# An early-fusion block in eight pairs of images: half of the gate on GpSimd, one rotation for three token tiles, narrower key windows, new orders

## What is computed

```
h = concat(cls, patches @ W_lin + b, txt) (+ positions)             # 16 x 165 x 256
q, k, v = rope(n @ Wq), rope(n @ Wk), n @ Wv      n = layernorm(h)  # 16 query heads, 4 key heads, 16 wide
scores = q k / 4, where |i - j| <= 32, else -inf  ; h += softmax(scores) v @ Wo
xq = int8 per token of layernorm(h);  w1, w2 to -1, 0, 1 times a scale
u = conv3(xq @ w1)  (3 taps along the tokens, 1024 channels)
g = silu(u);  h += (int8 per token of g) @ w2
```

## Time and profile before

| | us |
|---|---|
| three runs | 435.99, 437.55, 438.02 (median 437.55) |
| profiled execution, own time | 435.96 |
| its span | 434.2 |
| DVE busy | 313.8 (72%) |
| ACT busy | 277.2 (64%) |
| POOL busy | 219.7 (51%) |
| PE busy (ends modelled) | 357.3 (82%) |

### The profile page before, as it was taken

How to read it: one execution, slowest core, us unless ns; L and a number is a source line. 1 busy time by engine, 2 the same in 40 slices (tenths; PEclk the granted TensorE clock), 3 DMA queues, 4 the chain that set the end, 5 groups by cost and what they waited for, 6 DMA issues and landing times.

```text
span 434.2 us, 8318 instructions
## 1 busy us (share of the span) xinstructions
PE 357.3 (82%) x2920; PEld 274.9 (63%) x2920; DVE 313.8 (72%) x644; ACT 277.2 (64%) x523; POOL 219.7 (51%) x244
## 2 busy tenths in 40 slices
PE   1683998997999697998997799899998998936533
PEld 1452776776787486667775687688667766824423
DVE  1147548754599766887897689859976997899972
ACT  2240356776788755876976698679757966661812
POOL 2306379698389623994499309961983016010000
PEclk9998899997899989999999999999999999985956
DMA  8671051000000010001000100010001000000011
GB/s 232 154 169 24 19 203 27 1 18 10 2 1 2 2 39 22 18 17 33 2 13 14 33 0 11 17 33 0 19 10 31 2 2 15 20 2 0 0 32 31
DMA packets 17788, 13.86 MB, mean 32 GB/s; under 512 B 10109, under 2 KB 16698, under 8 KB 17747
## 3 DMA queue, kind: packets, MB, share of 16 engines
q1 hardware_dynamic: 16852, 12.18, 10.9%
q10 hardware_dynamic: 895, 1.16, 1.0%
HBM read 7.91 MB, written 2.70 MB: 24 GB/s over the span
## 4 chain that ended last, share of the span: by engine, by line
POOL 37%; PE 27%; DVE 11%; issue 10%; ACT 5%; DMA 5%; SPq 3%; POOLq 0%; ACTq 0%; DVEq 0%
POOL qkr L1064 7%; POOL rsn L1059 5%; POOL rc L1057 5%; POOL shared L1084 5%; POOL qsp L1076 5%; PE bank L1635 3%; POOL qsp L1072 3%; SPq L996 3%; PE bank L1842 2%; PE bank L1821 2%; DMA cst<-in_consts 2%; POOL shared L1092 2%; POOL qsp L1073 2%; PE bank L1736 2%; POOL rs L1035 2%
## 5 line engine op out<-in xcount | busy, mean ns | idle before, releaser
L1190 ACT COPY pT<-bank 94x480 f32<-94x480 f32 x88 | 49.0, 557 | 20.1 <-PE bank L1754 20.0
L1408 DVE TENSOR_REDUCE mx<-bank 120x4 fp32r<-120x376 f32 x88 | 47.2, 542 | 18.2 <-PE bank L1736 18.2
L1736 PE MATMUL bank<-kbd,q_hl 128*120 128x376 f32 x176 | 57.2, 410 | 0.0
L1754 PE MATMUL bank<-cst,pr 120*94 120x120 f32 x352 | 52.1, 270 | 2.7 <-ACT pT L1190 1.7
L1035 POOL TENSOR_TENSOR rs<-ve,half_neg 110x3 f32<-110x3 f32 x16 | 15.4, 962 | 75.2 <-DVE ve L1436 43.5
L1182 ACT ACTIVATE pr<-bank 120x376 f32<-120x376 f32 x88 | 42.7, 488 | 16.2 <-PE bank L1744 15.4
L1226 ACT ACTIVATE shared<-bank,conv 128x330 f32<-128x330 f32 x64 | 39.4, 633 | 12.3 <-PE bank L1822 11.5
L1821 PE MATMUL bank<-xT_hi,w1T 128*128 128x330 f32 x128 | 45.4, 360 | 2.1 <-DVE shared L1491 1.7
L1484 DVE SCALAR_TENSOR_TENSOR shared<-bank,conv,shared 128x328 f32<-128x328 f32 x64 | 35.3, 555 | 13.9 <-ACT shared L1226 13.2
L1754 PEld LDWEIGHTS bank<-cst,pr 120*94 120x94 f32 x352 | 37.6, 126 | 11.0 <-issue 5.2
L1042 POOL TENSOR_SCALAR xn<-h,mv,rs 110x256 f32<-110x256 f32 x21 | 29.0, 1387 | 25.6 <-PE bank L1674 25.1
(11 more groups left out here) (120 smaller groups left out, 854.8 us busy)
## 6 DMA issues: line engine op xcount, KB each, us to landing
out<-h SPq DMA_DIRECT2D x8, 330.0 KB
wn<-in_w SPq DMA_DIRECT2D x2, 1024.0 KB, 6.7
shared<-in_x SPq DMA_DIRECT2D x4, 432.0 KB
vw<-qk SPq DMA_DIRECT2D x40, 23.5 KB
h<-in_txt SPq DMA_DIRECT2D x1, 770.0 KB
wlT<-in_lin SPq DMA_DIRECT2D x1, 768.0 KB, 7.2
h<-tokp SPq DMA_DIRECT2D x14, 36.0 KB
h<-in_txt SPq DMA_DIRECT2D x1, 448.0 KB
```

The costliest lines, as they stand in the source:

```text
L1190: nc.scalar.copy(pT[:, g % 3, :], PT_BANK[0:KW, 0:HKV * QP]).then_inc(p_kept, 1)
L1408: nc.vector.tensor_reduce(mx[:, g % 4, :].bitcast(F32R), S_BANKS[g % 2][0:QP, 0:HKV * KW].rearrange("p (k c) -> p k c", k=HKV), axis=AX.X, ...
L1736: o = nc.tensor.matmul(dst, q_hl[n % 2][:, j * QB:(j + 1) * QB, :].bitcast(F32R), kbd[n % 2][:, part, :, k0:k0 + KW].bitcast(F32R), start= ...
L1754: o = nc.tensor.transpose(PT_BANK[0:KW, kv * QP:(kv + 1) * QP], pr[:, g % 3, kv * KW:(kv + 1) * KW], ident[0:QP, 0:QP])
```

## The change

1. **Gate.** The first half of `silu` leaves DVE. POOL makes it in two products over 128x1320, th*u and then that plus u. `abs_g` of the first half waits for POOL. The second half stays on DVE.
2. **Rotation.** From pair 1 on, one call of `rope` handles all three token tiles: 7 instructions of three times the columns in place of 21. It waits for the last `keep_qk`, and every `turn_q` waits for all of it. In pair 0 nothing changes (one tile on POOL, two on DVE).
3. **Keys.** Each block gets the keys that it can see: widths 62, 92, 94, 94, 78, 94, 78, 94, 94, 92, 62 in place of 94 (mean 84.9). The mask is added after the two products and only over the columns at the edges (29 to 94 of each key head, mean 56.2, so 225 in all).
4. **Orders.** Every row of `ORDER` and `ONCE` is new.

```
-            def rope(n, t):
...
+            def rope(n, ts, parts, added, high, split, before):
+                cnt = ts.stop - ts.start
...
+                pool.wait_ge(qk_kept, NT * n + ts.stop)
...
+                nc.gpsimd.tensor_tensor(rot[:, ts, :].rearrange("p t (h d) -> p t h d", h=heads), q_v, table(0), ALU.mult)
+                nc.gpsimd.tensor_tensor(swp[:, ts, :].rearrange("p t (h d) -> p t h d", h=heads), q_v, table(1),
+                                        ALU.mult).then_inc(parts, 1)
...
                 for e in range(2):
-                    o = nc.gpsimd.tensor_tensor(qkr[:, e::2], rc[:, e::2], rsn[:, 1 - e::2], ALU.add)
+                    o = nc.gpsimd.tensor_tensor(rot[:, ts, e::2], rot[:, ts, e::2], swp[:, ts, 1 - e::2], ALU.add)
...
+            def silu_first(n):
+                pool.wait_ge(tanhed, NP * n + 1)
+                nc.gpsimd.tensor_tensor(th[:, 0:HALFC, :], th[:, 0:HALFC, :], u[:, 0:HALFC, :], ALU.mult).then_inc(gate_mult, 1)
+                pool.wait_ge(gate_mult, n + 1)
+                nc.gpsimd.tensor_tensor(u[:, 0:HALFC, :], th[:, 0:HALFC, :], u[:, 0:HALFC, :], ALU.add).then_inc(gated_p, 1)
...
             def abs_g(n, p):
-                act.wait_ge(silued, NP * n + p + 1)
+                act.wait_ge(gated_v if p else gated_p, n + 1)
...
             def turn_q(n, t):
-                pe.wait_ge(q_split[t], n + 1)
+                if n:
+                    pe.wait_ge(q_split, n)
...
-                nc.tensor.matmul(dst, identb[0:QP, 0:QP], mask_v[:, j, :].unsqueeze(1).to_broadcast([QP, HKV, KW]),
-                                 start=True, stop=False)
                 for part in range(2):
-                    o = nc.tensor.matmul(dst, q_hl[n % 2][:, j * QB:(j + 1) * QB, :].bitcast(F32R),
-                                         kbd[n % 2][:, part, :, k0:k0 + KW].bitcast(F32R), start=False, stop=(part == 1))
+                    nc.tensor.matmul(dst, q_hl[n % 2][:, j * QB:(j + 1) * QB, :].bitcast(F32R),
+                                     kbd[n % 2][:, part, :, k0:k0 + w].bitcast(F32R), start=(part == 0), stop=(part == 1))
...
+                nc.tensor.matmul(over, identb[0:QP, 0:QP], hide,
+                                 start=False, stop=True, skip_group_check=True).then_inc(scored, 1)
```

More of the change, by code:

```diff
@@ L69, with keys_of, edges @@
 POSR = NPATCH + 1
-def key_start(j):
-    return min(max(QB * j - HALF_WINDOW, 0), T - KW)
+def keys_of(t):
+    lo = t // SEQ * SEQ
+    return max(t - HALF_WINDOW, lo), min(t + HALF_WINDOW + 1, lo + SEQ)
+SEEN = [[keys_of(t) for t in range(QB * j, QB * (j + 1))] for j in range(NB)]
+KEY0 = [min(lo for lo, hi in seen) // 2 * 2 if j < NB // 2 else min(lo for lo, hi in seen) for j, seen in enumerate(SEEN)]
+WIDTH = [-(-(max(hi for lo, hi in seen) - k0) // 2) * 2 for seen, k0 in zip(SEEN, KEY0)]
+def edges(j):
+    lo, hi = max(lo for lo, hi in SEEN[j]) - KEY0[j], min(hi for lo, hi in SEEN[j]) - KEY0[j]
+    if lo >= hi:
+        return 0, 1, WIDTH[j]
+    left, right = lo, WIDTH[j] - hi
+    if not left:
+        return hi, 1, right
+    if not right:
+        return 0, 1, left
+    return 0, 2, max(left, right)
+MASK_AT = [0]
+for _j in range(NB):
+    MASK_AT.append(MASK_AT[-1] + edges(_j)[1] * edges(_j)[2])
 def tok_pieces(s):
@@ L345 @@
-        (332,),
-        (369,),
+        (46,),
+        (89,),
+        (137,),
+        (184,),
+        (234,),
+        (280,),
+        (322,),
+        (359,),
     ),
     'dve.max_x': (
-        (48,),
-        (94,),
-        (143,),
-        (192,),
-        (242,),
-        (289,),
-        (338,),
-        (375,),
+        (51,),
+        (96,),
+        (145,),
+        (193,),
+        (239,),
+        (288,),
+        (331,),
+        (367,),
     ),
     'dve.low_x': (
-        (57,),
+        (56,),
@@ L360 @@
         (104,),
-        (152,),
-        (200,),
-        (249,),
-        (297,),
-        (345,),
-        (379,),
+        (153,),
+        (201,),
+        (247,),
+        (295,),
+        (342,),
+        (372,),
     ),
     'dve.left': (
[8 rows of a table removed]
[8 rows of a table added]
     ),
     'dve.right': (
[8 rows of a table removed]
[8 rows of a table added]
+    ),
+    'dve.fold_g': (
+        (74, 86),
+        (123, 134),
+        (174, 182),
+        (224, 230),
+        (268, 274),
+        (318, 325),
+        (364, 368),
+        (395, 397),
+    ),
+    'dve.max_g': (
+        (82, 87),
+        (131, 136),
+        (179, 183),
+        (225, 231),
+        (272, 278),
+        (319, 326),
+        (366, 369),
+        (396, 398),
@@ L447 @@
+        (194, 196, 197),
+        (241, 242, 243),
+        (289, 291, 292),
+        (337, 339, 340),
+        (385, 392, 393),
+        (402, 403, 404),
     ),
@@ L630 @@
         (4,),
+        (6,),
         (9,),
[L632 to L636 removed]
+        (15,),
+        (22,),
+        (29,),
+        (41,),
     ),
     'pool.rstd2': (
[L639 to L646 removed]
+        (11,),
+        (18,),
+        (25,),
+        (32,),
+        (37,),
+        (44,),
+        (48,),
+        (52,),
     ),
     'pool.norm2': (
[L649 to L655 removed]
+        (12,),
+        (19,),
+        (26,),
+        (33,),
+        (38,),
+        (45,),
+        (49,),
         (),
@@ L658 @@
     'pool.dequant_x': (
-        (17,),
-        (25,),
-        (33,),
-        (41,),
-        (48,),
-        (55,),
-        (58,),
-        (),
+        (13,),
+        (21,),
+        (27,),
+        (34,),
+        (40,),
+        (46,),
+        (50,),
+        (),
+    ),
+    'pool.silu_first': (
+        (16,),
+        (23,),
+        (30,),
+        (35,),
+        (42,),
+        (47,),
+        (51,),
+        (53,),
     ),
@@ L671 @@
         (7,),
-        (9,),
+        (10,),
+        (12,),
+        (14,),
+        (16,),
+        (18,),
+    ),
+    'sp.store': (
+        (8,),
         (11,),
@@ L710, in times_of @@
         return [(t, k) for k, t in enumerate(ONCE[name])]
-    return [(t, (n, k)) for n in range(PAIRS) for k, t in enumerate(ORDER[name][n]) if t is not None]
+    return [(t, (n, k)) for n, row in enumerate(ORDER[name]) for k, t in enumerate(row) if t is not None]
 TICKS = sorted({t for name in (*ORDER, *ONCE) for t, _ in times_of(name)})
@@ L1108, in _ @@
                     dequant_x(n)
-                for n, t in work["rope"].get(q, ()):
-                    rope(n, t)
+                for n, _ in work["rope"].get(q, ()):
+                    rope_pair(n)
+                for n, _ in work["silu_first"].get(q, ()):
+                    silu_first(n)
         @block.scalar
@@ L1586, in _ @@
                     right(n, m)
-                for n, p in work["silu"].get(q, ()):
-                    silu(n, p)
+                for n, _ in work["silu"].get(q, ()):
+                    silu(n, 1)
                 for n, p in work["fold_g"].get(q, ()):
```

688 lines of the change are left out of this document (323 added, 365 removed), and 176 rows, old and new, of the table ORDER.

## The result

The changed kernel takes **467.93 us** (median of four runs, 466.63 to 469.80) against 437.11 for the kernel before on the same chip: ratio 1.071, 95% interval 1.0664 to 1.0755. It is 30.8 us slower; 434.5 was forecast, in a range of 425 to 443. The span of the profiled execution is 466.2 us. Two kernels of the experiments, the rotation in 21 pieces and the one with the gate in pieces too, have one execution each in a slower state (466.49 and 474.74 us) in their medians.

The account below looks back on a forecast made before the run. No engine is full; POOL's rotation turns the chain, 42.3 us a turn. Terms +2.4 - 3.3 - 1.2 - 1.5 - 3.0 + 1.8 + 1.8 = -3.0 from 436.0 give 433.0, 434.5 on the median's scale; range 425 to 443.

Parts of the forecast that it names:

- load_v behind store: On SP, load_v(n+3) waiting behind store(n) costs 1 to 2 us at pair 5's copies, covered because the gate holds POOL.
- The other new orders I put at 0, between -2 and +2: The other new orders of the start, priced at 0, between -2 and +2 us.
- the convolution order: In the convolution of pairs 1 to 4, DVE works off fewer attention pieces: -1.8 us a turn, nothing if ACT doesn't keep up.
- Gate and rotation, +2.7 a turn before the offsets: On POOL, both together take 20.5 us in a turn that had 17.8; with offsets -1.0, +1.5 and -0.8, +2.4.
- Rival 1: POOL's queue is the turn and the convolution order gives nothing back: +9.6 instead of +2.4, 441.8 us; chance 0.26.
- rival 2: DVE instructions wait for longer POOL instructions to end: +1.2 us in five pairs, 440.5 us; chance 0.08.
- The merged rotation "3.5 of the 4.4" for DVE's work: On POOL, 3.5 of 4.4 us of hand-overs and stretching stay; with 11.0 for the merged call, 14.5 in place of 17.8.
- Pair 1's rotation, +1.8: The only rotation the scores wait for; merged, it ends 11.0 us after the last keep_qk instead of 4.5: +1.8, between 0 and 6.5.
- Keys, -4.5 in sum: Narrower keys shorten attention blocks: -3.3 us where attention is alone, -1.2 in the turns; gain between 0 and 17.6.
- Rival 4: The keys don't get cheaper: 4.5 us less gain, 439.0 us at most, 437 if half of it; chance 0.08.
- DVE, -4.5 for the lost gates: DVE loses eight gates: -1.5 us in pair 0's feed-forward part, -3.0 in pairs 5 and 6; bounds 0 and -12.2.
- The end, +1.8: In pair 7, the gate on POOL, despite an earlier tanh, delays the end: +1.8 us, bounds 0 and +3.5.

Follow-up runs that it names:

- the base: The changed kernel with SP's order of before (value copies of pair n+3 ahead of the store of pair n): 459.64 us, 1.0513 against the kernel before.
- experiment 6: Kernel before with new orders only up to the first turn_xs: 434.94 us; order edits on it (452.07) and on the changed kernel without its gate, rotation and SP edits (468.46, 445.13).

## Why the prediction was wrong

- **The step that failed** is the one that set new orders at nothing. In the prediction's words, load_v behind store "costs 1 to 2 us at that place, but the gate holds POOL until 264.4 anyway; cover: the gate". The length of the copies (12.7 us), their landing 2.0 after, and the wait that follows were right: 1.5 to 2.2 us in three of the four turns. What it holds was wrong: not only POOL, but ACT, and behind `keep_qk` on ACT the `mid` of the pair in its feed-forward part. The cover was named for one waiter out of two, the wait in the first of the four turns is 6.75, and the delay closes a ring through `add_ffn` and `store`. Price 8.3 us, not 0.
- **"The other new orders I put at 0, between -2 and +2"**, and the convolution order at -1.8 a turn. The -1.8 never came: in the base the last `right` of pairs 1 to 4 ends 22.7, 18.6, 18.9 and 17.5 us after `turn_xs`, before it was 21.0, 19.2, 18.0 and 18.8, on average 0.2 later. I counted what left the convolution and not where it went. The start gives 2.3 (shown). The rest of the orders costs some 15 (13 with the start's gain in it); of these 4.8 are the places of stats1 and of the gate on DVE, shown in a kernel whose gate is on DVE. About 10 stay open: in the four turns they lie mostly behind the last `right` (experiment 6), but no run took their causes apart, and the two that tried made it worse.
- **Gate and rotation, +2.7 a turn before the offsets.** The durations were right. Rival 1's mechanism, POOL's queue as the turn, is shown under the old orders (4.6 us for the gate alone in the turn that was read). In the changed kernel it isn't what turns: POOL has 9% of the chain. The 9.7 us of both are there all the same, and they go by DVE: 11.7 of the 13.9 us that four turns lose stand in six DVE instructions.
- **The lock, rival 2.** The mechanism is shown, and 6 us were too few: shorter instructions on POOL, with more work in sum, take 10.7 us from five turns, and 11.0 from the six DVE instructions in four of them. Those six take 6.8 us in pair 3 before and 9.4 in pair 3 after. I gave it 0.08 and treated it as a rival of the forecast, where it is a term in every turn.
- **The merged rotation "3.5 of the 4.4" for DVE's work.** It takes 12.9 to 14.0 us in the turns (14.5 forecast), 11.0 undisturbed in pairs 1 and 2 (11.0 forecast). Right.
- **Pair 1's rotation, +1.8.** Wrong in sign: `turn_xs(0)` stands at 109.5 in the base and at 111.2 with the rotation in tiles, so merging gains 1.7 there, or 0.5 with the gate on DVE (110.7 and 111.2).
- **Keys, -4.5 in sum.** Rival 4 has the time right (0.9995, an interval around 1) and the mechanism wrong. The instructions did get shorter (a score product takes 300 ns at 248 columns and 353 at 312, 410 before at 376), the path did not; why not even pair 0's attention gained (`turn_xs(0)` at 113.3 in place of 113.9) stays open.
- **DVE, -4.5 for the lost gates.** None of it shows: DVE's busy time rose by 1.3 in place of falling by some 15, and pairs 5 and 6 take 1.7 us more than before (65.9 against 64.2).
- **The end, +1.8.** From `turn_xs(7)` to the end of the span 40.4 us in place of 38.7: +1.7, the number right. The reason is in part luck: with the gate back on DVE in the new orders the end still takes 39.5 us, or 40.3 with the rotation in tiles too.
- **Signs to look for.** The lengths of the products and POOL's idle time between gate and rotation in pairs 1, 2 and 4 (8.0, 2.0 and 2.6 us, and 2.7 in pair 3 too): right. POOL above 60%: wrong, 51% (its 239.4 us would be 55% of the forecast span). The chain through POOL: wrong, 9%. Turns of 42 to 43.5: wrong, 50 to 53.

No single rival was the result. In the order in which the experiments took it apart, it is the sum of a ring that I saw and priced at nothing (8.3), gate and rotation (9.7), and orders whose cost I did not look for (13, with the start's gain).

## What to carry to other kernels

When a step is put behind another in an in-order queue, follow every waiter of what it issues, on each engine, to what stands behind it, and ask whether the way leads back to the step it now waits for: that is a ring, and while it is closed no turn is shorter than it. Fewer, longer instructions on GpSimd save fixed cost (11.0 us against 13.0 for the same rotation with little beside it), and here they held VectorE longer (11.0 us in four turns) and handed over later: look at what VectorE does beside them before merging. Take a large reordering apart by stretches before judging it: here the first 110 us were a gain and the rest a loss.

## What the runs showed of the hardware

- DVE and POOL stretch each other in both directions. The rotation in 21 pieces takes 13.0 us in pair 2 and 15.1 in pair 1, where DVE works on 128x2048 elements beside it (1.29 and 1.76 us) and the three low parts take 4.54 in place of 2.49; in seven instructions it is 11.0 in both pairs. A 128x660 fold on DVE takes 0.84 to 2.81 us by what POOL does beside it.
- GpSimd's product is close to linear in columns over the range seen: 320 in 0.87, 960 in 2.16 to 2.24, 1320 in 2.96 to 3.00.
- TensorE stood still for 5.1 us: its granted clock was 0.67 on average from 68 to 72 us, 0.50 from 72 to 76, with PE at work for 3.65 of these 4 us, and 0.97 from 76 to 80.
